# Moving a chunk's square root, first two query tiles and a bias product to other half-steps of a fused attention and expert kernel

## What is computed

```python
x = x + attention(layernorm(x))    # 16 heads of 16 channels, rotary embedding, softmax over 1024 keys
xc = bf16(layernorm(x)); nf = bf16(xc * rsqrt(mean(xc*xc) + eps) * norm_weight)
logits = nf @ gate.T; the two best of 8 experts, weighted by a softmax over their two logits
p1 = nf @ mlp1[e]; act = g * sigmoid(1.702 g) * (lin + 1), g and lin clipped at 7
p2 = act @ mlp2[e] + bias2[e]
x = x + bf16(xc + bf16(sum over e of combine[e] * p2[e]))
```

## Time and profile before

| what | us |
|---|---|
| median of 3 runs | 1120.46 |
| lowest and highest of them | 1111.45, 1121.25 |
| the profiled execution | 1118.18 |
| its span, first to last instruction | 1116.4 |
| TensorE busy | 940.6 |
| VectorE busy | 774.1 |
| ScalarE busy | 747.5 |
| GpSimd busy | 422.0 |

### The profile page before, as it was taken

How to read it: one execution, slowest core, us unless ns; L and a number is a source line. 1 busy time by engine, 2 the same in 40 slices (tenths; PEclk the granted TensorE clock), 3 DMA queues, 4 the chain that set the end, 5 groups by cost and what they waited for, 6 DMA issues and landing times.

```text
span 1116.4 us, 16572 instructions
## 1 busy us (share of the span) xinstructions
PE 940.6 (84%) x5217; PEld 400.6 (36%) x5288; DVE 774.1 (69%) x1529; ACT 747.5 (67%) x1017; POOL 422.0 (38%) x356
## 2 busy tenths in 40 slices
PE   4629899789888997989889998889989999996564
PEld 1412222234343443334343443334433443344243
DVE  4751211488858886588858786588867886786897
ACT  2417886777668785777668785777768887881232
POOL 2423302533264424544264434543331332334252
PEclk9758999899999998999999998999999999998587
DMA  4353536244435343444534343444534453421110
GB/s 162 99 111 78 117 82 130 67 105 115 111 91 137 88 114 86 110 103 103 125 84 125 97 110 81 107 104 105 125 78 114 105 125 88 99 91 39 48 47 29
DMA packets 79988, 109.81 MB, mean 98 GB/s; under 512 B 22531, under 2 KB 56723, under 8 KB 76819
## 3 DMA queue, kind: packets, MB, share of 16 engines
q1 hardware_dynamic: 61460, 83.47, 32.1%
q10 hardware_dynamic: 18432, 25.17, 7.6%
HBM read 82.90 MB, written 25.69 MB: 97 GB/s over the span
## 4 chain that ended last, share of the span: by engine, by line
PE 54%; DVE 17%; issue 10%; ACT 7%; DMA 4%; POOL 3%; SPq 2%; ACTq 1%; another core or an unknown queue 0%; DVEq 0%; POOLq 0%
PE OP L698 15%; PE S L684 14%; PE D L670 8%; ACT probs L815 4%; PE D L574 4%; PE BB L653 3%; PE A L653 3%; PE D L596 3%; DVE th_sb L1118 2%; DMA o_scr<-O 2%; DVE acc L1113 2%; DVE l_sb L1103 2%; DVE g_sb L1101 2%; PE D L588 2%; ACT sqs L778 1%
## 5 line engine op out<-in xcount | busy, mean ns | idle before, releaser
L815 ACT ACTIVATE probs<-S 128x1024 f32<-128x1024 f32 x512 | 513.3, 1025 | 170.1 <-PE S L684 169.4
L684 PE MATMUL S<-Qs,Ks 98*128 98x512 bf16 x1024 | 302.5, 388 | 35.6 <-ACT probs L815 19.9
L698 PE MATMUL OP<-probs,V 128*17 128x512 f32 x2048 | 276.1, 612 | 3.6 <-ACT O L824 3.6
L899 POOL TENSOR_TENSOR act_lo<-act_sb,act_hi 128x512 fp32r<-128x512 f32 x128 | 171.2, 1340 | 150.4 <-ACT act_hi L804 148.2
L684 PEld LDWEIGHTS S<-Qs,Ks 98*128 98x128 bf16 x1024 | 79.0, 99 | 217.0 <-ACT probs L815 100.4
L670 PE MATMUL D<-W,act_hi 128*128 128x256 f32 x448 | 131.9, 327 | 25.6 <-issue 14.1
L1113 DVE SCALAR_TENSOR_TENSOR acc<-D,combh,acc 128x256 f32<-128x256 f32 x224 | 97.6, 476 | 79.0 <-PE D L670 78.6
L1118 DVE SCALAR_TENSOR_TENSOR th_sb<-th_sb,g_sb 128x512 f32<-128x512 f32 x128 | 121.8, 951 | 16.9 <-ACT th_sb L791 13.1
L893 POOL TENSOR_SCALAR W<-W2b 128x512 fp32r<-128x512 bf16 x64 | 43.6, 681 | 198.6 <-PE D L670 193.4
L670 PE MATMUL D<-W,act_lo 128*128 128x256 f32 x448 | 113.4, 285 | 0.0
L804 ACT CAST act_hi<-act_sb 128x512 fp32r<-128x512 f32 x128 | 78.3, 612 | 52.0 <-DVE act_sb L1123 49.3
(11 more groups left out here) (137 smaller groups left out, 1002.4 us busy)
## 6 DMA issues: line engine op xcount, KB each, us to landing
W<-in_w ACTq DMA_DIRECT2D x64, 256.0 KB, 2.8
Ks<-k_scr SPq DMA_DIRECT2D x32, 384.0 KB
W2b<-in_w ACTq DMA_DIRECT2D x64, 128.0 KB, 2.8
Ks<-k_scr SPq DMA_DIRECT2D x32, 256.0 KB
o_scr<-O SPq DMA_DIRECT2D x32, 256.0 KB, 4.3
q_scr<-parts SPq DMA_DIRECT2D x16, 384.0 KB, 3.5
k_scr<-parts SPq DMA_DIRECT2D x16, 384.0 KB, 2.5
Qs<-q_scr SPq DMA_DIRECT2D x32, 192.0 KB
```

What stands on the lines that cost most here:

```text
L684: last = mm(S[:, j2, C * i:C * (i + 1)], Ks[0:SROWS + MROWS, g % 2, j, P * kt:P * (kt + 1)], Qs[0:SROWS + MROWS, g % 2, j, :], start=True, ...
L698: last = mm(OP[32 * j:32 * j + VW, :], V[:, kt, HG * g + j, :], probs[:, s % 2, C * j:C * (j + 1)], start=kt == 0, stop=kt == KT - 1)
L815: nc.scalar.activation(probs[:, s % 2, 2 * C * j2:2 * C * (j2 + 1)], S[:, j2, :], ACT.Exp, scale=SCALE).then_inc(exp_done, 1)
L899: tt(act_lo[:, e % 2, it, :], act_sb[:, a % 2, :], act_hi[:, e % 2, it, :].bitcast(FP32), ALU.subtract).then_inc(lo_s, 1)
```

## The change

- rstd1 moves from half-step 1 to 3, and xn from 4 to 5.
- qk0 moves from half-step 10 to 11 and qk1 from 12 to 15, each with its chain.
- GpSimd's part of the length stage becomes a stage of its own, r1, still at +5. The rest of length (TensorE, VectorE) lies at +6 for tiles 0 and 1 and at +5 for tiles 2 and 3.
- b21 moves from half-step 34 to 36.
- In TensorE's exact block the eight groups written out become a hardware loop of four over two groups.

For tiles 0 and 1 the half-steps become:

| stage | tile 0 | tile 1 |
|---|---|---|
| qk | 10 to 11 | 12 to 15 |
| rope | 12 to 13 | 14 to 17 |
| part1 | 13 to 14 | 15 to 18 |
| r1 | 15 to 16 | 17 to 20 |
| length | 15 to 17 | 17 to 21 |
| part2 | 17 to 18 | 19 to 22 |
| part3 | 20 to 21 | 22 to 25 |

```diff
-    AT = {"x_next": 8, "stats1": 1, "rstd1": 1, "xn": 4, "xT0": 7, "xT1": 8, "qk0": 10, "qk1": 12, "qk2": 22,
-          "qk3": 30, "rope": 2, "part1": 3, "length": 5, "part2": 7, "part3": 10, "v0": 37, "v1": 42, "gmax": 1,
+    AT = {"x_next": 8, "stats1": 1, "rstd1": 3, "xn": 5, "xT0": 7, "xT1": 8, "qk0": 11, "qk1": 15, "qk2": 22,
+          "qk3": 30, "length": 5, "v0": 37, "v1": 42, "gmax": 1,
...
-          "combT": 32, "b20": 33, "b21": 34}
+          "combT": 32, "b20": 33, "b21": 36}
...
-        for st in ("rope", "part1", "length", "part2", "part3"):
-            place(PREP, h + AT[st], (st, a))
+        for st, after in (("rope", 2), ("part1", 3), ("r1", 5), ("length", 5 + (a < 2)), ("part2", 7), ("part3", 10)):
+            place(PREP, h + after, (st, a))
...
-            HEAD += [("length", *tile[2]), ("part2", *tile[2]), ("part3", *tile[2])]
+            HEAD += [("r1", *tile[2]), ("length", *tile[2]), ("part2", *tile[2]), ("part3", *tile[2])]
...
-                    for n in range(NCH):
-                        for g in range(NG):
-                            wait_apart(pe, (ex_ld[g % 2], EX_STACK * (4 * b + 2 * n + g // 2 + 1)))
+                    with pe.Fori(0, NCH * NG // 2) as pair:
+                        for slot in range(2):
+                            wait_apart(pe, (ex_ld[slot], EX_STACK * (4 * b + 1) + EX_STACK * pair))
                             with pe.Fori(0, HG) as j:
                                 for t in range(TC):
-                                    wait_apart(pe, (ex_red, 128 * b + 16 * (NG * n + g) + t + 1 + TC * j))
+                                    wait_apart(pe, (ex_red, 128 * b + 16 * slot + t + 1 + 32 * pair + TC * j))
...
-                elif st == "length":
+                elif st == "r1":
                     pool.wait_ge(qk_p1, 4 * u + a + 1)
                     tt(sw[:, a % 2, :], rot[:, a % 2, :], parts[:, a % 2, 0, :], ALU.subtract).then_inc(qk_r1, 1)
```

More of the change, by code:

```diff
@@ L720, in turn @@
                         wait_apart(pe, (exp_done, NCH * PAIRS * b))
-                    for n in range(NCH):
-                        for g in range(NG):
-                            wait_apart(pe, (ex_ld[g % 2], EX_STACK * (4 * b + 2 * n + g // 2 + 1)))
+                    with pe.Fori(0, NCH * NG // 2) as pair:
+                        for slot in range(2):
+                            wait_apart(pe, (ex_ld[slot], EX_STACK * (4 * b + 1) + EX_STACK * pair))
                             with pe.Fori(0, HG) as j:
                                 for t in range(TC):
-                                    wait_apart(pe, (ex_red, 128 * b + 16 * (NG * n + g) + t + 1 + TC * j))
+                                    wait_apart(pe, (ex_red, 128 * b + 16 * slot + t + 1 + 32 * pair + TC * j))
                                     for hf in range(2):
                                         last = mm(S[:, t % 2, C * hf:C * (hf + 1)],
-                                                  Qs[0:SROWS, g % 2, bass.ds(j, 1), P * t:P * (t + 1)].rearrange("k o t -> k (o t)"),
-                                                  Ks[0:SROWS, g % 2, bass.ds(j, 1), C * hf:C * (hf + 1)].rearrange("k o t -> k (o t)"),
+                                                  Qs[0:SROWS, slot, bass.ds(j, 1), P * t:P * (t + 1)].rearrange("k o t -> k (o t)"),
+                                                  Ks[0:SROWS, slot, bass.ds(j, 1), C * hf:C * (hf + 1)].rearrange("k o t -> k (o t)"),
                                                   start=True, stop=True)
```

## The result

The changed kernel takes 1156.49 us (median of 4 runs, 1155.75 to 1159.02) against 1118.26 us for the kernel before, run beside it: a ratio of 1.036, 95% interval 1.033 to 1.040. That is 38 us slower by the two medians. The forecast was 1128.5 us with a range up to 1142: it had the right side, but a fifth of the loss (8 us), and "within 1%" had the larger chance. The profiled execution took 1156.39 us, its span is 1154.6 us.

The account below looks back on a forecast made before the run. It took TensorE, busy 940.6 of 1116.4 us, as the bound, its idle time to be won or lost. Terms -20.6 + 12.8 + 3.5 + 1.2 + 13.7 - 1.0 = +9.6 us; 8 added to the 1120.46 median gave 1128.5, range 1103 to 1142.

Parts of the forecast that it names:

- within 1%: Whole kernel: a time from 1109 to 1131.7 us, about what cannot be told from no change; chance 0.48.
- code of the exact block, r1: TensorE's exact block: its code is skipped before and after, so 0 us.
- square root: Chunks 2 to 5, first half-steps: moving rstd1 behind the lo stage ends TensorE's stall, 20.6 us less.
- tiles, all chunks: Later tiles 0 and 1: 12.8 us more in chunks 2 to 5, 3.5 in chunk 0, 1.2 in chunk 1.
- b21: b21 at 36 waits 2.8 us for nsq: 13.7 us more in chunks 1 to 5, 1.0 less in 6 and 7.
- rival D: Where chunks 2 to 5 begin: the stall is no GpSimd wait and stays, 1150 us; chance 0.03.
- VectorE is about 0.6 us behind: Chunk 2, second transpose: VectorE's lag from xn and one xnT copy, within the 11.3 us from down to down.
- Rival C: Start of chunks 2 to 5: VectorE takes the stall over, 2.5 us slip, gain 10.6 us, 1138.5 us; chance 0.14.
- Three chances in four for the clock: b21 in chunks 2 to 5: chance that the 2.8 us wait lowers the clock, costing another 1.4 us.
- A: Tiles and b21: the waits come but are short of the clock, sum +0.2, 1120 us; chance 0.20.
- B: Stall, bank D and b21 waits all go, nothing is late: 1080 us, half 1100 us; chance 0.18 with its half.

Follow-up runs that it names:

- the tiles alone: The code alone with qk0 at 11, qk1 at 15 and length of tiles 0 and 1 one half-step later: 1150.62 us, ratio 1.032 to the kernel before.
- the code alone: Changed kernel with all half-steps as in the kernel before, keeping only the exact block's loop and r1 as its own step: 1114.51 us, ratio 1.0002 to before.
- the square root alone: The code alone with rstd1 moved from half-step 1 to 3 and xn from 4 to 5: 1104.42 us, ratio 0.991 to the kernel before.
- run (d): The square root alone with qk0 at 9, qk1 at 11, length of tiles 0 and 1 six behind, VectorE's statistics at 0: 1107.81 us, ratio 0.993 to before.
- the shuffle first: Changed kernel with tile 1's rotation ahead of tile 0's length at half-step 17, no half-step moved: 1137.76 us, ratio 1.020 to the kernel before.

## Why the prediction was wrong

Most of its mechanisms were right, its sizes not; one loss, in quarters where nothing was moved, it did not have at all. Step by step:

| term | predicted | measured by itself |
|---|---|---|
| code of the exact block, r1 | 0 | 0 |
| square root | -20.6 | -10.4 |
| tiles, all chunks | +17.5 (12.8 + 3.5 + 1.2) | +36 |
| b21 | +12.7 (13.7 - 1.0) | +17 |
| sum | +9.6 | +43 (the change itself: +38) |

**The tiles: the step that failed.** It is the term of 12.8 + 3.5 + 1.2 us, and in it what a lower clock costs: 1.3 us a chunk, for one pair of score products (1.03 us against 0.60) and the value products behind it (1.84 us against 1.05), and nothing at all outside the quarter of the wait. The mean change a chunk in chunks 2 to 5, in us, read from the starts of these products and copies in the runs with the tiles alone and with the code alone:

| stretch | predicted | measured |
|---|---|---|
| up to the down of half-step 10 | 0 | -0.4 |
| from there to the down of 16 | -2.6 | -1.9 |
| from there to the score product of 21 | +3.9 | +3.9 |
| from there to the end of the second quarter | +1.9 | +2.7 |
| third quarter | 0 | +2.4 |
| sum | +3.2 | +6.7 |

The working up to the wait held: TensorE waits 4.6 us there (4.7 predicted), by the chain that the prediction wrote out. Ahead of it, the two qk products did not become shorter, which had been counted as 0.5 us: they take 1.98 us each in the kernel after, as before. Behind it, the clock stayed low through the length product, the next scores and qk2 as well: in the kernel after the durations of the five groups from 351.20 add up to 7.2 us, where their likes at full clock make 4.5 (0.60, 1.05, 0.39, 0.60 and 1.88).

The largest piece is the third quarter, for which the prediction had nothing. The windows of it in chunk 3, with the code alone, then with the tiles alone:

```profile
483.70:516.10 32.40, 29.48 (x173) 13.42 (x174) 28.16 (x44) 23.49 (x33) 15.93 (x14) 1.00 0.36 99
```

```profile
504.60:539.90 35.30, 32.37 (x173) 14.02 (x175) 28.27 (x44) 23.43 (x32) 15.87 (x14) 0.90 0.32 93
```

The same 173 matmuls, 2.9 us of idle time in both, and 2.9 us more of busy time at the lower clock. The wait ahead of b21 in it is 1.64 us in the first and 1.65 us in the second. With the tiles alone the granted clock is 0.50 from 510.38, where b21 starts behind that wait, to 516.50; with the code alone it is 1.00 from 487.00 to 494.00. So in these executions, one of each kernel, a wait behind which the clock stayed up otherwise is followed by the lower level once the tiles have moved. The granted clock is 0.95, 0.90, 0.95 and 0.90 in the third quarters of chunks 2 to 5, against 1.00 in all four with the code alone. How the move does this is not shown. In the eleven kernels of this document with b21 at 34, all 44 third quarters of chunks 2 to 5 follow this number: 31.6 to 32.4 us at a granted clock of 1.00, 33.2 to 34.0 at 0.95, 34.6 to 35.4 at 0.90.

In chunk 0 it was 8.4 us, not 3.5: ScalarE's wait for GpSimd is 2.45 us (some 3 predicted), but TensorE's own wait behind it is 4.06 us and its products take 4.1 us longer at a granted clock of 0.83, of which the prediction counted nearly nothing. In chunk 1 it was 5.1 us, not 1.2. These pieces add up to 40 us; the profiled run is 36 us longer, with 1.8 us less ahead of the first copy and 3 less behind the last. The tiles are 18 of the 33 us between the predicted sum and that of the parts. The bound failed as well: 4.5 us a chunk was put as the worst.

**The square root.** Right: the stall was GpSimd's wait for the variance (no "issue" is left, rival D is out), and its gain was under the whole wait. Wrong: 11.3 us from down to down was 14.1 when it ran alone. "VectorE is about 0.6 us behind" did not reckon with longer instructions: xn took 1.95 us instead of 1.38 and a fused product 1.65 us instead of 0.69, and the wait came out at 1.84 us, with the clock down behind it. Rival C was built for this and priced at a slip of 2.5 us, a gain of 10.6 us; the run gave 10.4. It was the right rival with too small a chance. That the two numbers agree so well is partly luck: by the quarters some 14 us were won and 5 lost again to the clock in the third quarters, which C did not have.

**b21.** The wait (2.69 for 2.8 us), its cause (nsq) and the lower clock behind were right in all of chunks 1 to 5 (0.50 to 0.57 in the 2.1 to 2.9 us of products right behind the wait, b21 alone). Three chances in four for the clock were one too few, chunk 1 grew by 3.1 us instead of 1.9, and the shrinking of chunks 6 and 7 didn't come. 17 us against 12.7.

**From the sum to the forecast.** 8 of 9.6 us were added on the ground that the waits had no slack behind them. They had none; they had a tail. Discounting a sum of waits was a mistake in the wrong direction.

**The range.** The errors of the three terms had one sign, and each hangs in part on one thing: how often and how long TensorE's clock is low. In the square root's, VectorE's longer instructions have a share as well. The rivals A and B let that go to nothing; none let it be double.

## What to carry to other kernels

Where TensorE is busy nearly all the time, price a new wait of it with the slow products behind it: here a quarter whose wait grew from 0.7 to 4.6 us got 7.7 us longer, and cutting 2.4 us from a wait gave back 6.2. Look also at the quarters that you did not touch: a wait there that was harmless can be followed by the lower clock once the work ahead of it has moved, and that was worth 2.4 us a chunk here. When a stage is moved to a half-step where another stage already stands, look first at the order of the two in each engine's queue; putting the one that feeds a long chain ahead of the one that only frees a bank was worth 18 us and moved nothing else. And try each part of such a change by itself: here one of three was worth 10 us, and the two others hid it.

## What was not expected

**A wait of 1.65 us sometimes brings the clock down and sometimes doesn't.** In the run with the square root alone, TensorE waits 1.65 us ahead of b21 in chunk 2 and in chunk 3, by the same code:

```profile
359.99 0.50 PE L623 MATMUL D<-b2f,combT 16*128 16x256 f32 x2 [1.65 <-DVE acc L1036]
...
481.88 0.79 PE L623 MATMUL D<-b2f,combT 16*128 16x256 f32 x2 [1.65 <-DVE acc L1036]
```

The windows of the two quarters (length, busy engines, clock):

```profile
353.90:385.80 31.90, 29.12 (x170) 13.21 (x173) 27.54 (x41) 23.46 (x32) 15.80 (x14) 1.00 0.42 107
474.00:509.20 35.20, 32.46 (x171) 13.83 (x173) 28.61 (x44) 23.05 (x31) 15.40 (x12) 0.90 0.35 90
```

The first ran at 1.00 and took 31.9 us, the second at 0.90 and 35.2 us: 3.3 us for a wait of equal length. In the rows shown here for chunks 2 to 5, waits of 0.97 us and less left the clock alone, and those of 1.65 to 1.84 us went either way (1.84 us ahead of xT0 was followed by scores of 1.06 us with the square root alone and of 0.60 us in the kernel after). Those of 2.64 us and more were followed by the lower level, at once or, behind the 2.64 us, after the first pair: the value products took 1.31 us and the next pair 1.03, at a granted clock of 0.62 from 345.00 to 347.50 and 0.50 from there to 350.00. But the length of a wait does not settle it even there. In chunk 1 of run (d) TensorE waits 2.79 us, and a little later 1.92 us at the place of the earlier trace rows, and the clock stays at 1.00 behind both:

```profile
198.99 1.99 PE L596 MATMUL D<-wo_sb,Op 128*128 128x256 f32 x8 [2.79 <-DVE X1s L1004]
...
205.08 0.60 PE L684 MATMUL S<-Qs,Ks 98*128 98x512 bf16 x2 [1.92 <-ACT probs L815]
```

```profile
198.90:208.00 9.10, 6.47 (x34) 2.56 (x36) 4.17 (x15) 5.14 (x9) 6.28 (x6) 1.00 0.25 59
```

So the 1.92 us of the earlier trace rows, on which the prediction leaned for the clock, is no bound either: the same wait at the same place went both ways. Where the quarters of one kernel jump by 1 to 3 us between executions, the granted clock was different in each of the three that I looked at, and that is a likely reason why the ratio of a small change needs many runs.

**VectorE's centring took 3.41 us instead of 1.5.** In the kernel after it runs beside GpSimd's sine product (343.92 and 344.10 in the rows above); in the kernel before it had GpSimd's rest product beside it for a part of its time only and took 1.46 us:

```profile
334.79 1.46 DVE L1011 TENSOR_SCALAR xc<-X1s,mv,rstd 128x256 bf16<-128x256 f32 x4
```

That is 1.95 us more for the same four instructions. The fused product of line 1123 shows a difference of the same kind: in the timelines of the kernel before it takes 0.69 us each of the 104 times that no GpSimd instruction runs beside it; of the 24 times that one does, 16 take 1.64 to 1.68 us, one 2.73, four 0.98 and three 0.69. What joins the two engines in this is not shown. Over the run VectorE is busy for 19.8 us more with the same instructions (793.9 - 774.1), and this is the largest piece that I found of it: by the grouped lines the 32 of them take 21.2 us after and 11.3 us before. The same instructions show it in every kernel where I looked: in each of chunks 2 to 5 they take 1.46 to 1.47 us before and with the square root alone, 3.4 us with the tiles alone and with tile 1 alone at 15, and 2.7 us with the shuffle first; in chunks 6 and 7, without PREP, 1.38 us everywhere. It feeds ScalarE's squares, which stand ahead of the exponential that TensorE waits for, but it is not what they waited for in chunk 2 after: it ends at 347.33, and ScalarE is busy with part1 until about 348.
